# Routing of the lead: stationary gate weights, and a second choice spread over GRU steps

## The reference, cut to what matters

```python
# layer 0: Sinkhorn plan of x, routed FFN on it
u, v = sinkhorn(exp(-x / 0.1), r, c)                 # 31 iterations
p = u * K * v                                        # (B, N, D)
scores = sigmoid(p @ gate_weight.T)                  # (T, 8 experts)
sfc = scores + gate_bias
# 2 groups of 4 experts: the sum of a group's two best decides the group;
# in it the two best experts are taken, ties to the lower index
topk_w = 2.5 * scores[topk] / (sum(scores[topk]) + 1e-20)
r2 = relu(p @ up) ** 2                               # 8 experts of 64, shared 256
x = x + sum_e(cw[:, e] * (r2_e @ down_e)) + shared(p)
# layer 1: GRU over the 32 positions, then attention and a mixture of experts on its output
for t in range(32):
    z = sigmoid([x_t, h] @ Wz + bz); r = sigmoid([x_t, h] @ Wr + br)
    c = tanh([x_t, r * h] @ Wh + bh)
    y_t = (1 - z) * h + z * c                        # next h: y_t, or tanh(y_t @ Wp + bp) each 4th
y = y + msa(layernorm(y, ln1)); y = y + moe(layernorm(y, ln2))
x = x + y
```

## Time and profile before

| | us |
|---|---|
| median of 3 runs | 496.57 (496.02 to 497.24) |
| the profiled execution | 496.99, its span 495.3 |
| TensorE busy in the span | 472.5 (95%) |
| VectorE busy | 348.8 (70%) |
| ScalarE busy | 324.1 (65%) |
| GpSimd busy | 234.7 (47%) |

### The profile page before, as it was taken

The page is one execution under the profiler, slowest core; times in us unless marked ns, Lnnn a source line. Parts: engine busy times, 40 slices in busy tenths (PEclk is TensorE's granted clock), DMA queues, the critical chain, the costliest instruction groups (busy, mean ns, idle before and its releaser), DMA issues. The chain is left out here.

```text
span 495.3 us, 24307 instructions
## 1 busy us (share of the span) xinstructions
PE 472.5 (95%) x9142; PEld 393.8 (80%) x9142; DVE 348.8 (70%) x1268; ACT 324.1 (65%) x808; POOL 234.7 (47%) x579
## 2 busy tenths in 40 slices
PE   8999999999999999999999998789999988999996
PEld 6899999999977545666666677678888877999996
DVE  6888888888877575766657656477888887734443
ACT  5455555556546963656665666577877768987773
POOL 3244444444453001055443554643477775777454
PEclk9999999999999999999999999999999999999999
DMA  5170000000000075143424000022233344555300
GB/s 177 45 257 0 0 0 0 0 0 0 0 2 2 28 162 130 42 77 85 86 54 123 1 1 2 31 63 71 64 118 111 122 139 148 167 162 153 98 30 27
DMA packets 23394, 34.42 MB, mean 69 GB/s; under 512 B 4096, under 2 KB 14341, under 8 KB 23208
## 3 DMA queue, kind: packets, MB, share of 16 engines
q1 hardware_dynamic: 20560, 27.23, 20.3%
q0 software_dynamic: 2784, 6.56, 3.7%
HBM read 23.88 MB, written 8.26 MB: 65 GB/s over the span
## 5 line engine op out<-in xcount | busy, mean ns | idle before, releaser
L206 ACT ACTIVATE den_v<-ps_g,floor 128x128 f32<-128x128 f32 x124 | 45.5, 367 | 38.9 <-PE ps_g L266 32.4
L266 PE MATMUL ps_g<-buf_a,u_pad 128*32 128x128 f32 x1984 | 66.7, 274 | 0.0
L280 PE MATMUL ps_g<-buf_b,v_pad 128*32 128x128 f32 x1984 | 63.7, 275 | 0.2
L266 PEld LDWEIGHTS ps_g<-buf_a,u_pad 128*32 128x32 f32 x1984 | 52.1, 110 | 2.6 <-issue 0.3
L280 PEld LDWEIGHTS ps_g<-buf_b,v_pad 128*32 128x32 f32 x1984 | 50.2, 109 | 1.8 <-DVE v_pad L374 0.5
L1433 POOL DMA_INDIRECT out<-buf_d,token_i x39 | 38.5, 988 | 23.8 <-DVE buf_c L1940 17.2
L374 DVE RECIPROCAL v_pad<-ps_g 128x32 f32<-128x32 f32 x124 | 38.8, 333 | 15.6 <-PE ps_g L272 13.5
L767 PE MATMUL ps_h<-buf_c,up 128*128 128x512 f32 x96 | 49.1, 607 | 0.6 <-DVE buf_c L1046 0.4
L192 POOL TENSOR_SCALAR held_u<-inv_u 128x8 f32<-128x8 f32 x124 | 23.8, 192 | 45.5 <-DVE inv_u L383 45.4
L1649 PE MATMUL ps_ss<-xT,buf_d 128*128 128x128 f32 x312 | 41.4, 276 | 0.0
L1649 PEld LDWEIGHTS ps_ss<-xT,buf_d 128*128 128x128 f32 x312 | 37.9, 192 | 0.4 <-ACT xT L1775 0.2
(11 more groups left out here) (360 smaller groups left out, 1253.3 us busy)
## 6 DMA issues: line engine op xcount, KB each, us to landing
cw_b<-cw_d SPq DMA_DIRECT2D x16, 512.0 KB, 7.6
buf_c<-sorted_x SPq DMA_DIRECT2D x39, 136.0 KB, 2.2
buf_a<-in_x SPq DMA_DIRECT2D x8, 256.0 KB, 5.2
buf_d<-in_x_nt SPq DMA_DIRECT2D x1, 2048.0 KB, 9.7
state<-buf_a SPq DMA_DIRECT2D x16, 128.0 KB, 2.0
x<-in_w SPq DMA_DIRECT2D x8, 256.0 KB, 3.1
buf_b<-in_w SPq DMA_DIRECT2D x8, 256.0 KB, 3.2
sorted_x<-nobody SPq DMA_DIRECT2D x1, 1088.0 KB, 11.0
```

Of the source, the lines that this page charges most:

```text
L206: fn(den_v[:, h, :], ps_v[h], ACT.Relu, bias=floor[:, h:h + 1]).then_inc(v_den, 1)
L266: last = mm(ps_v[h][32 * j:32 * j + 32, :], u_pad[:, h, j, 32 * i:32 * i + 32], K[:, t * D:(t + 1) * D], start=i == 0, stop=i == TI - 1)
L280: last = mm(ps_u[h][32 * c:32 * c + 32, :], v_pad[:, h, c, 32 * i:32 * i + 32], KT[:, b * N:(b + BG) * N], start=i == 0, stop=i == TI - 1)
```

## The change

**The logits** are made the other way round: the gate weights, padded with zeros to 32 columns, are stationary, and 512 tokens move. Four quarters go to the four column groups of the array, so one part of four quarters is four matmuls, with experts on the partitions (32 to a quarter). The sigmoid is taken there, and VectorE's transposes of 32x32 blocks bring the scores to tokens on partitions, and the weights back afterwards. The turns of the weights on TensorE and the copies out of PSUM are gone. `cw_d` is written by one DMA a quarter, four for each part.

**The lead's order** changes on TensorE: logits(0) after the sixth turn of u, the outputs between ups 9 and 23 and not in two blocks. On VectorE part 0 is ranked after four products of `pt_n`, and the other four come behind it.

**Part 1** is ranked in the lead only up to the choice of the group. Its other 17 steps, and the transpose, are cut into six parts that stand in the GRU's steps 0 to 5, between `kept` and the wait for the candidate's gate. SyncE's wait for them stands where the wait for part 1 stood, behind `repeat(2)`.

**LN1's tail**: statistics of steps 28 and 29 move ahead of `fresh`, and ScalarE levels steps 28 and 29 while VectorE levels 30 and 31. A new clear of `cw` is GpSimd's first instruction.

```diff
@@ sync
-                sp.wait_ge(w_first, 1)
-                sp.dma_start(cw_d[:, 0:W], cw_t[:, 0:W]).then_inc(w_out, 16)
-                sp.wait_ge(w_out, 16)
+                def send_weights(q, done):
+                    part, j = divmod(q, QS // PARTS)
+                    sp.dma_start(cw_d[:, q * W:(q + 1) * W], cw_t[32 * j:32 * j + E, part, :]).then_inc(done, 16)
+
+                sp.wait_ge(w_turned, 1)
+                send_weights(0, w_out0)
+                for q in range(1, QS // 2):
+                    send_weights(q, w_out)
+                sp.wait_ge(w_out0, 16)
                 repeat(0)
-                sp.wait_ge(w_first, 4)
-                sp.dma_start(cw_d[:, W:4 * W], cw_t[:, W:4 * W]).then_inc(w_out, 16)
-                sp.wait_ge(w_out, 32)
+                sp.wait_ge(w_out, 48)
                 repeat(1)
                 for q in range(2, QS):
                     sp.wait_ge(gated, S.last_gate[q - 2])
                     repeat(q)
                     if q == 2:
-                        sp.wait_ge(w_second, 4)
-                        sp.dma_start(cw_d[:, 4 * W:T], cw_t[:, 4 * W:T]).then_inc(w_out, 16)
-                        sp.wait_ge(w_out, 48)
+                        sp.wait_ge(w_turned, 2)
+                        for late_q in range(QS // 2, QS):
+                            send_weights(late_q, w_out)
+                        sp.wait_ge(w_out, 112)
@@ gpsimd
+                g.memset(cw[:], 0.0).then_inc(cleared, 1)
...
                 def keep_step(n):
                     if n == 0:
-                        pool.wait_ge(w_out, 48)
+                        pool.wait_ge(w_out0, 16)
+                        pool.wait_ge(w_out, 112)
@@ tensor
-                def logits(q):
...
+                def logits(part):
+                    pe.wait_ge(pt_ready, (part + 1) * QS // PARTS)
+                    for j in range(QS // PARTS):
+                        q = part * (QS // PARTS) + j
+                        last = mm(ps_l[part][32 * j:32 * j + 32, :], gate_w[:], pt_n[:, q * W:(q + 1) * W], start=True, stop=True)
                     last.then_inc(l_mm, 1)
@@ scalar
+                    for part, at in enumerate((4, 18)):
+                        if p == at:
+                            act.wait_ge(l_mm, part + 1)
+                            fn(scores_t[:, part, :], ps_l[part][:], ACT.Sigmoid).then_inc(scored, 1)
...
                 normed(TAIL // 2 - 2)
                 normed(TAIL // 2 - 1)
+                act.wait_ge(st.shifted, 1)
+                for n in (TAIL, TAIL + 1):
+                    act.wait_ge(st.b_mm, (n - st.SLOTS) // 2 + 1)
+                    fn(st.xh[:, n % st.SLOTS, :], st.rows[:, n % st.SLOTS, :], ACT.Identity, scale=st.scale[:, n:n + 1],
+                       bias=st.shift[:, n:n + 1]).then_inc(st.level, 1)
                 normed(TAIL // 2)
@@ vector
+                def rank(part):
                     dve.wait_ge(scored, part + 1)
+                    c.step(v.transpose(scores[:].rearrange("p n e -> p (n e)"), scores_t[:, part, :]))
...
+                def find():
+                    c.step(v.tensor_reduce(top[:], biased[:], AX.X, ALU.max))
+                    c.step(tt(eq[:], biased[:], top[:, :, None].broadcast_to(wide), ALU.is_equal))
+                    c.step(tt(eq[:], eq[:], prefer[:, None, :].broadcast_to(wide), ALU.mult))
...
+                def hand_over(part):
+                    c.step(v.reciprocal(top[:], top[:]))
+                    c.step(v.scalar_tensor_tensor(out=cw[:, :, 0:E], in0=cw[:, :, 0:E], scalar=2.5,
+                                                  in1=top[:, :, None].broadcast_to(wide), op0=ALU.mult, op1=ALU.mult))
+                    v.transpose(cw_t[:, part, :], cw[:].rearrange("p n e -> p (n e)")).then_inc(w_turned, 1)
...
                     c.step(tt(quarters(kept), h, quarters(zh), ALU.subtract))
+                    if t >= TAIL + 2:
+                        spread(t - 2)
+                    if t == N - 1:
+                        aggregate(TAIL)
+                        aggregate(TAIL + 1)
+                    if t in (0, 2):
+                        find()
+                    if t in (1, 3):
+                        mark(t // 2)
+                    if t == 4:
+                        share()
+                    if t == 5:
+                        hand_over(1)
                     dve.wait_ge(c_done, t + 1)
```

More of the change, by code:

```diff
@@ L588, in plan_ffn_gru @@
         ps_u = ps_c
[L589 to L590 removed]
+        ps_l = (ps_z, ps_r)
         ps_ut = ps_y[0][:, 0:N]
@@ L746, in spread_u @@
                     last.then_inc(u_mm, 1)
-                def logits(q):
-                    part, first = divmod(q * STEPS, TP)
-                    for k in range(STEPS):
-                        n = q * STEPS + k
-                        last = mm(ps_l[part][:, first + k, :], pt_n[:, n * B:(n + 1) * B], gate_w[:], start=True, stop=True)
-                    last.then_inc(l_mm, 1)
-                def turn_weights(q):
-                    if q >= 4 and q < 7:
-                        pe.wait_ge(w_first, q - 3)
-                    for k in range(STEPS):
-                        last = nc.tensor.transpose(ps_w[q][0:E, k * B:(k + 1) * B], cw[:, q * STEPS + k, :], ident[:])
-                    last.then_inc(w_mm, 1)
+                def logits(part):
[3 more added lines that the diff above has]
+                        last = mm(ps_l[part][32 * j:32 * j + 32, :], gate_w[:], pt_n[:, q * W:(q + 1) * W], start=True, stop=True)
+                    last.then_inc(l_mm, 1)
                 def hidden(p):
@@ L857, in turn_back @@
                 def turn_back(pair):
-                    pe.wait_ge(st.level, 2 * pair + 2)
+                    if pair == N // 2 - 1:
+                        pe.wait_ge(st.level_last, 2)
+                    else:
+                        pe.wait_ge(st.level, 2 * pair + 2)
                     for k in range(2):
@@ L1038, in spread, with aggregate, times_u @@
                     v.bn_stats(st.six[:, n, :], st.rows[:, n % st.SLOTS, :]).then_inc(st.stats, 1)
-                times_v(0)
-                for c in range(CHS):
-                    if 1 <= c and c + 1 < CHS:
-                        times_v(c + 1)
+                def aggregate(n):
+                    dve.wait_ge(st.stats, n + 1)
+                    c.step(v.bn_aggr(st.mean_var[:, n - TAIL, :], st.six[:, n, :]))
+                def times_u(c):
                     dve.wait_ge(u_mm, c + 1)
@@ new lines, in mark @@
+                def mark(n):
+                    c.step(v.tensor_reduce(top[:], eq[:], AX.X, ALU.max))
+                    c.step(tt(hot[:, n], eq[:], top[:, :, None].broadcast_to(wide), ALU.is_equal))
+                    if n == 0:
+                        c.step(v.scalar_tensor_tensor(out=biased[:], in0=hot[:, 0], scalar=-1e30, in1=biased[:],
+                                                      op0=ALU.mult, op1=ALU.add))
+                    else:
+                        c.step(tt(hot[:, 0], hot[:, 0], hot[:, 1], ALU.add))
@@ L1092, in _ @@
                 dve.wait_ge(early.pref, 1)
                 dve.wait_ge(early.gate_in, 32)
-                for part in range(PARTS):
-                    weigh(part)
+                dve.wait_ge(cleared, 1)
+                rank(0)
+                find()
+                mark(0)
+                find()
+                mark(1)
+                share()
+                hand_over(0)
+                times_u(4)
+                for n in range(5, CHS):
+                    times_v(n)
+                    times_u(n)
@@ L1099, in _ @@
                         gating(p)
-                for q in range(QS // 2, QS):
-                    dve.wait_ge(w_mm, q + 1)
-                    v.tensor_copy(cw_t[:, q * W:(q + 1) * W], ps_w[q][0:E, :]).then_inc(w_second, 1)
+                rank(1)
                 add(0)
@@ L1132, in _ @@
                         add(n)
-                def aggregate(n):
-                    dve.wait_ge(st.stats, n + 1)
-                    c.step(v.bn_aggr(st.mean_var[:, n - TAIL, :], st.six[:, n, :]))
-                for n in range(TAIL, N - 2):
-                    aggregate(n)
                 spread(N - 2)
```

120 lines of the change are left out of this document (52 added, 68 removed).

## The result

The changed kernel takes **501.55 us** (median of 5 runs, 501.39 to 501.86) against 496.57 for the kernel before on the same chip: 1.0097 of its time, 95% interval 1.0082 to 1.0112. That is 4.98 us more, where the forecast of 498.9 was 2.3 more. The profiled execution took 501.76 us with a span of 500.0, against 495.3 before, so its trace has 4.7 us to explain.

The account below looks back on a forecast made before the run. TensorE's own work and its waits were taken to bound the kernel up to the GRU's end. Terms -7.9 + 1.4 + 7.35 + 1.8 - 0.3 = +2.35 on the 496.57 us median gave 498.9 us, range 497.9 to 500.6.

Parts of the forecast that it names:

- The lead, -7.9: Lead before the GRU: less TensorE matmul work for logits and weight turns saves 7.9 us (-8.8 to -6.5).
- The replay of the queues: Lead: engine queues followed in order, up 20 starting at 172.95, first multiply done at 173.3, weights from DRAM just hidden.
- The parts, +1.4: GRU steps 0 to 5: six parts of the second choice delay steps 0, 2 and 3, +1.4 us (+0.7 to +1.9).
- The stall, +7.35: GRU step 6: VectorE's multiply waits for the late spread of quarter 3, and TensorE with it, +7.35 us (6.4 to 8.4).
- The clock, +1.8: Behind the stall: TensorE's clock falls and some 3.6 us run at half rate, +1.8 us (0 to +3.6).
- The tail, -0.3: LN1's tail: ScalarE levels steps 28 and 29 beside VectorE's 30 and 31, -0.3 us (-0.7 to +0.2).
- The work behind it is unchanged: Behind the GRU stall: work stays the same and TensorE was full there, so nothing of the 7.35 us is caught up.
- at no cost: GRU: GpSimd's first copy waits till 213.5 for the late weights' DMAs; its rows, read in step 8, cost nothing.
- Rival A: GRU step 6: quarter 3's weights arrive in time, no stall, only -6.8 us left, so 489.8 us; 12% chance.

Follow-up runs that it names:

- e1: Changed kernel with SyncE sending the second ranking's weights behind the spread of quarter 3 instead of ahead of it: 492.70 us, 0.991 of the kernel before.
- e2: Changed kernel with 30 unread 128-column identity matmuls in step 7 ahead of TensorE's wait for rh: 498.26 us, ratio 1.0027 to the kernel before.
- e10: e1 with 120 more TensorE instructions (small matmuls) just ahead of the third block: 491.64 us, 0.9884 of the kernel before.
- e11: Kernel before with 96 more TensorE instructions (small matmuls) just ahead of the third block: 500.65 us, ratio 1.0069.
- e9: e4 with GpSimd's copies of y of steps 0 to 3 behind the first group's levels, and 120 more TensorE instructions ahead of the third block: 491.89 us, 0.9894.
- e3: Changed kernel with all six parts of the second choice done in the lead behind the second ranking, none in the GRU: 497.34 us, ratio 1.0005.
- e4: e1 with the first two of the six parts in the lead and the others in steps 1, 4 and 5: 492.21 us, 0.9917.
- e5: e1 with TensorE's program 160 instructions longer at its start (42 small matmuls for two of eight warm-up ones): 495.68 us.

## Why the prediction went wrong where it did

Direction and chain were right; the size was 2.6 us short. By its steps:

- **The lead, -7.9.** Measured -7.64 in the changed kernel, and -7.62 to -7.66 in e1, e2 and e10 once the Sinkhorn's end, which moves by up to 0.9 us between builds with the same Sinkhorn and start (e11 against e9), is taken off. The replay of the queues held to 0.3 us, the weights' chain too: up 20 was due at 172.95 and began at 173.40, 0.31 of it the Sinkhorn's; the first multiply, due to be done at 173.3, began at 173.14 and still ended ahead of its output at 174.36.
- **The parts, +1.4.** Measured 1.37: 0.48, 0.21 and 0.67 in steps 0, 2 and 3, nothing in 1, 4 and 5. The sum was better than its terms (0.5, 0.5, 0.4): steps 2 and 3 missed by 0.3 each, in opposite directions, and that they cancel is luck.
- **The stall, +7.35.** Measured 7.47, and e1 shows that it is SyncE's order alone.
- **The clock, +1.8.** Measured 2.27 (2.2 by e2). TensorE worked at the lower level for 4.8 us behind the gap (0.53 over 5.10 us in the windows above), where I had taken 3.6 from the program's start. The mechanism was right, the term 0.47 too small. The warning of the Trainium skill ("TensorE: Matmul & The Clock Gate", HAM oscillation), matmuls that wait on a DMA come back throttled, is what the trace shows: clock 0.53 from 218.0 to 223.1.
- **The tail, -0.3.** Measured -0.11; TensorE waits 0.98 us for ScalarE's pairs, which begin only when ScalarE is through with the turned rows.
- **The failed step: "The work behind it is unchanged".** The sum ended with the tail and took the third block as a copy of the old one. It was a copy in code, not in place: the block costs 1.24 us more, with a wait of 0.78 us that comes and goes with the length of TensorE's program: the removed matmuls moved the boundaries at which its instructions arrive. This is the largest part of the miss, and nothing in the sum stood for it. The rest is the clock (0.5), the lead (0.3, and 0.3 of a Sinkhorn that ended later), the tail (0.2) and the stall (0.1), less 0.2 that the later GRU steps won back.
- **What was hidden:** GpSimd's copy, "at no cost". True with the stall, 0.7 us without it.

Rival A (the weights are there in time) described what e1 is, not what this change is: e1 has -7.66 + 1.37 + 0.7 for GpSimd and the same third block.

## What to carry to other kernels

When work moves past an in-order queue, follow every transfer behind the new wait to its reader: here a gain of 7.6 us in the lead turned into a loss by one `wait` one loop turn too early on SyncE, and moving it made the kernel 0.9% faster than before instead of 1.0% slower. A gap on TensorE of 4.5 us or more is to be priced with the slow matmuls behind it, some 2 us here. And after instructions are taken out, compare the unchanged stages too: a wait marked "issue" ahead of a burst of small matmuls may be the instruction fetch, and a few dozen cheap instructions in an idle place moved it away (e10 against e1: 1.1 us by the medians, 0.9884 and 0.991 of the kernel before, with intervals that overlap; the traces show it, the times alone do not).

## What was not expected of the hardware

TensorE can wait for its own instructions with no branch between them and the work before: 0.5 to 1.2 us, in the first pass of a loop and in no later one (0.2 to 0.5 us at the start of a pass is another wait, and in the kernel before too), in front of matmuls that everything else had released, just behind 64 records of small matmuls in 1.07 us. The wait ended 2.4 to 2.7 us after a 16 KB instruction transfer began. It was there in the kernels with 160 records less and 96 more than the kernel before (under 0.2 us in two of them, whose clock was low), and not in those with 0 and 40 less. And the clock fell with less than the 7.4 us of the stall: with 4.49 us in e3, and in the third block of e4 and e5, where the longest wait ahead of the fall is 1.44 us. In e3 it fell 2.6 us after TensorE had stopped, in the changed kernel 5.3 us after.
